# The residual of three attention blocks: DVE's multiply-add replaced by a scaled copy on ScalarE and an accumulating DMA

## What is computed

```
mod = silu(c) @ wmod                        # six vectors per batch: sa ca ga sb cb gb
h   = layernorm(x) * (1 + ca) + sa
H   = tanh(relu(rope(h @ W_Q)) + hh_b)      # "attention": projection, rotation, relu, tanh
g   = groupnorm(H, 32 groups) * gn_weight + gn_bias
x2  = x + ga * reshape(transpose(g))        # tokens and channels swapped, then read as rows
h   = layernorm(x2) * (1 + cb) + sb
y   = x2 + gb * (silu(h @ Wg) * (h @ Wu)) @ Wd     # weights looked up in a table of 16 entries
```

## Time and profile before

| | us |
|---|---|
| median of three runs | 1021.43 |
| the profiled execution, its time | 1024.31 |
| its span, first to last instruction | 1022.5 |
| TensorE busy | 929.9 (91%) |
| VectorE busy | 605.7 (59%) |
| ScalarE busy | 430.9 (42%) |
| POOL busy | 142.9 (14%) |

### The profile page before, as it was taken

The page is one execution under the profiler, slowest core; times in us unless marked ns, Lnnn a source line. Parts: engine busy times, 40 slices in busy tenths (PEclk is TensorE's granted clock), DMA queues, the critical chain, the costliest instruction groups (busy, mean ns, idle before and its releaser), DMA issues.

```text
span 1022.5 us, 12879 instructions
## 1 busy us (share of the span) xinstructions
PE 929.9 (91%) x4364; PEld 435.0 (43%) x4364; DVE 605.7 (59%) x1375; ACT 430.9 (42%) x652; POOL 142.9 (14%) x131
## 2 busy tenths in 40 slices
PE   5569678868999989999999998999999999999998
PEld 1234334333444434444444444444444444444443
DVE  5799989995899973238988863412223432222312
ACT  3375847478777732255256223222223331222200
POOL 3311202032233321121022001010000110000000
PEclk9789788989999999999999998999999999999999
DMA  8658366721001032241523305140000203000001
GB/s 280 186 123 227 83 205 167 244 63 31 21 21 31 11 124 83 72 142 34 164 51 114 83 27 200 40 146 0 0 0 1 72 31 103 0 0 0 7 35 42
DMA packets 33738, 83.44 MB, mean 82 GB/s; under 512 B 2848, under 2 KB 2976, under 8 KB 30624
## 3 DMA queue, kind: packets, MB, share of 16 engines
q1 hardware_dynamic: 32544, 74.54, 22.1%
q0 software_dynamic: 1152, 8.39, 4.4%
HBM read 64.04 MB, written 18.87 MB: 81 GB/s over the span
## 4 chain that ended last, share of the span: by engine, by line
PE 68%; DVE 17%; issue 5%; ACT 5%; DMA 3%; POOL 1%; SPq 0%; DVEq 0%; ACTq 0%
PE ps L1187 34%; PE ps L1223 22%; DVE hid L840 4%; PE ps L1154 4%; DMA xa<-x_dram 3%; PE ps L1176 2%; DVE st L759 2%; PE ps L1142 2%; PE ps L1199 2%; DVE R L826 1%; POOL work L436 1%; ACT h L500 1%; ACT xa L490 1%; PE ps L1234 1%; DVE gs L747 1%
## 5 line engine op out<-in xcount | busy, mean ns | idle before, releaser
L1187 PE MATMUL ps<-h,w_all 128*128 128x512 f16 x1920 | 418.2, 380 | 3.3 <-ACT w_all L552 2.5
L1187 PEld LDWEIGHTS ps<-h,w_all 128*128 (+1 forms) x1920 | 188.1, 98 | 230.8 <-ACT w_all L552 3.0
L1223 PE MATMUL ps<-w_all,hid 128*128 128x512 f16 x1056 | 231.9, 382 | 0.4 <-DVE w_all L1069 0.4
L1223 PEld LDWEIGHTS ps<-w_all,hid 128*128 128x128 f16 x1056 | 103.9, 98 | 125.5 <-issue 3.8
L879 DVE SCALAR_TENSOR_TENSOR hd<-ps,col,sg 128x512 f32<-128x512 f32 x80 | 59.9, 749 | 129.1 <-ACT sg L522 128.7
L522 ACT ACTIVATE sg<-ps,col 128x512 f32<-128x512 f32 x80 | 54.7, 684 | 173.4 <-PE ps L1187 173.0
L904 DVE SCALAR_TENSOR_TENSOR hd<-ps,col,gbB 128x512 f32<-128x512 f32 x32 | 24.0, 751 | 145.2 <-PE ps L1223 144.8
L1154 PE MATMUL ps<-WQ,work 128*128 128x512 f16 x384 | 87.0, 385 | 14.4 <-POOL work L436 11.2
L490 ACT ACTIVATE xa<-xa,ln_sb 128x512 f32<-128x512 f32 x60 | 43.9, 803 | 123.1 <-DVE ln_sb L769 123.1
L1176 PE MATMUL ps<-hid,w_all 128*128 128x512 f16 x352 | 85.5, 403 | 9.6 <-DVE hid L840 8.6
L537 ACT ACTIVATE hid<-hd 128x512 f16<-128x512 f32 (+1 forms) x88 | 54.8, 626 | 88.0 <-DVE hd L879 69.5
(11 more groups left out here) (113 smaller groups left out, 765.6 us busy)
## 6 DMA issues: line engine op xcount, KB each, us to landing
R<-x_dram SPq DMA_DIRECT2D x16, 1024.0 KB, 6.9
xa<-x_dram SPq DMA_DIRECT2D x14, 1024.0 KB, 5.7
hid<-idx_dram SPq DMA_DIRECT2D x44, 256.0 KB, 5.7
R<-bias_dram POOLq DMA_DIRECT2D x8, 1024.0 KB, 8.7
out_dram<-R SPq DMA_DIRECT2D x32, 256.0 KB, 2.2
x_dram<-R SPq DMA_DIRECT2D x7, 1024.0 KB, 5.1
w_all<-wmod_dram SPq DMA_DIRECT2D x6, 1024.0 KB, 12.7
h<-idx_dram SPq DMA_DIRECT2D x11, 256.0 KB, 2.6
```

Of the source, the lines that this page charges most:

```text
L1187: ins = nc.tensor.matmul(bank(GU[2 * s + t]), W[wp][:, bass.ds(at, P)], h2[hp][:, s, k], start=(k == 0 and i == 0), stop=(k == K - 1 and i ...
L1223: ins = nc.tensor.matmul(bank(QY[par]), hid[hp][:, bass.ds(at, P)], W[wp][:, w_at:w_at + BLK], start=(j == 0 and i == 0), stop=(j == J - 1 ...
```

## The change

For q = 0, 1, 2 of batch 0 the residual leaves VectorE. ScalarE copies each transposed and weighted g tile from PSUM into a buffer of its own (`bias_rows[0]`, free once the bias matrix has been stored), and POOL issues one DMA of 1 MB that accumulates this buffer onto R. The buffer is reused by the next block after that DMA has landed. `x2_ready` is now counted by ScalarE for these blocks, and SP waits for the new semaphore `g_added` (the accumulating DMA has landed) before it stores R. On POOL the accumulation of g for block q stands behind the bias addition of block q + 1. The last block of batch 0 and all of batch 1 are as before.

```diff
@@ SP
                 if not last:
-                    sp.wait_ge(x2_ready, K * (q + 1))
+                    sp.wait_ge(g_added, 16 * (q + 1))
                     sp.dma_start(x2_of_block(0, q), R[q % 2].rearrange("p (q n) -> p q n", q=A)).then_inc(x2_out, 16)
@@ POOL
             split_lo(0, hq[0], hq[1])
+            def add_g_rows(q):
+
+                pool.wait_ge(x2_ready, K * (q + 1))
+                pool.wait_ge(rows_added[q % 2], 16 * (q // 2 + 1))
+                nc.gpsimd.dma_start(R[q % 2][:], bias_rows[0], accum_op=ALU.add).then_inc(g_added, 16)
+
+            add_bias_rows(0, 0)
             for q in range(NB - 1):
-                add_bias_rows(q, 0)
                 split_lo(q + 1, hq[0], hq[1])
-            add_bias_rows(NB - 1, 0)
+                add_bias_rows(q + 1, 0)
+                add_g_rows(q)
@@ ScalarE
+            def weighted_g(q):
+
+                if q:
+                    act.wait_ge(g_added, 16 * q)
+                else:
+                    act.wait_ge(bias_out, 16)
+                for k in range(K):
+                    act.wait_ge(gt_ready, K * q + k + 1)
+                    nc.scalar.activation(bias_rows[0][:, k * C:(k + 1) * C], bank(TB[k % 2]), ACT.Copy,
+                                         scale=gnw[:, k:k + 1]).then_inc(x2_ready, 1)
...
                 if not last:
                     summed_out(w + 3, 1)
+                    weighted_g(q)
                     half_idx(w + 6, 0)
@@ VectorE
                 if last:
                     dve.wait_ge(xt_ready, K * NB)
                     dve.wait_ge(x2_out, 16 * (NB - 1))
-                residual(q, half, (xa[:, A - 1], xb[:, A - 1]) if last else ())
+                    residual(q, half, (xa[:, A - 1], xb[:, A - 1]))
```

More of the change, by code:

```diff
@@ L204, in build @@
         mod_mm = sem("mod_mm"); mod_copied = sem("mod_copied"); gate_made = sem("gate_made")
+        g_added = sem("g_added")
         silu_c = sem("silu_c"); vec_mm = sem("vec_mm"); row_mm = sem("row_mm")
```

## The result

The change made the kernel slower. The median is 1039.11 us (four runs, 1038.5 to 1044.69) against 1021.2 us before (four runs by now); the ratio is 1.0179, 95% interval 1.0151 to 1.0207, so 15 to 21 us. The forecast was 1035 us, within 1028 to 1047.

The account below looks back on a forecast made before the run. The first stage was taken to be bound by VectorE and its waits, chiefly the load of x behind the residual. Terms 6.7 + 5.8 + 1.0 = 13.5 us, added to 1021.43, gave 1035 us, within 1028 to 1047.

Parts of the forecast that it names:

- Block 1, +5.8 us: End of block 1: g lands at 137.2 behind the bias, x at 144.9, against statistics of block 3 at 139.13: +5.8 us.
- What decides: Batch 0: the residual of block q opens the way to x for block q + 2, with 0.6 us or nothing to spare.
- VectorE's relief counted at 0: Start of blocks 1 to 3: 2.90 us each off VectorE turns into waiting for the projection; paying rival 8.7 us, chance 0.03.
- Block 0, +6.7 us: End of block 0: g lands at 94.2, x at 101.9, so the statistics of block 2 wait: +6.7 us.
- Block 2, 0: End of block 2: no load of x waits for its store, 6 us in hand: 0, bound +5 if transfers collide.
- the projection of block 3, +1.0 us: Start of block 3: ScalarE's copies make TensorE's projection start later, and VectorE with it: +1.0 us.
- Sum: Whole kernel: 6.7 + 5.8 + 1.0 = 13.5 us slower.
- An accumulation from SBUF: Rival, transfers of g: a copy from SBUF is quicker than from DRAM, two blocks gain 3.0 us each, about 1029; chance 0.06.
- The collision rival: g crawls behind bias and modulation weights, x meets index loads: the stage loses 20 to 34 us, about 1047; chance 0.10.
- stall of descriptors: Rival: POOL's descriptors of g held while VectorE writes masks, each g up to 2.76 us late, about 1039; chance 0.02.

Follow-up runs that it names:

- e1: Changed kernel with the load of x for block q + 2 issued ahead of the wait for g_added: 1028.62 us, ratio 1.0085 to the kernel before.
- e3: Changed kernel without the accumulating DMA of g, ScalarE's copies kept, R stored when they are done: 1028.1 us, ratio 1.0071 to the kernel before.
- e8: e5 with the load of x still earlier, before the last index load of the block: 1016.71 us, ratio 0.9966 to the kernel before.
- e9: e2 with the load of x at the same earlier place as in e8: 1019.35 us, ratio 0.9979 to the kernel before.
- e7: Changed kernel with the modulation weights of block 1 loaded behind the load of x for block 3: 1036.27 us, ratio 1.0171 to the kernel before.
- e4: Changed kernel with POOL issuing the accumulation of g ahead of the next block's bias addition: 1043.94 us, ratio 1.0224 to the kernel before.
- e6: Changed kernel with ScalarE's weighted copies ahead of the last copy of table sums: 1036.21 us, ratio 1.0148 to the kernel before.
- e10: e1 with eight useless matmuls in TensorE's idle time between transpose groups two and three of blocks 0 to 2: 1024.34 us, ratio 1.0044 to the kernel before.
- e2: Kernel before with the load of x moved ahead of the wait for the residual: 1017.89 us, ratio 0.9974 to the kernel before.
- e5: e1 with ScalarE's weighted copies ahead of the last copy of table sums: 1022.46 us, ratio 1.0009 to the kernel before.

## Why the prediction was right, and where it was off

The mechanism and the sign came as forecast, and the time lies 4 us above the 1035. The term that was mis-sized most is the one of block 1, +5.8 us, which measured +8.94.

- *What decides.* That the load of x hangs on the residual through SP's program order, and that the change therefore puts an accumulating DMA in front of it, held: e1 and e3, which cut this link in two different ways, each take away more than half of the loss.
- *VectorE's relief counted at 0.* Right, with the cover named: the projection. Even with every wait for x gone (e8) the 2.90 us a block reappear as idle time; what may be left of them there is under 1 us in the traces and 1 to 3 us in the runs of e8 against e9.
- *Block 0, +6.7 us.* Measured +7.24. g landed after 7.8 us (8.0 assumed), x after 7.4 (7.3 assumed). ScalarE's copy out of PSUM took 0.69 us (0.73 assumed). The bias ahead of it cost nothing that shows here: it was down at 85.3, 1.3 us after the issue of g.
- *Block 1, +5.8 us.* Measured +8.94: the term that was mis-sized. I let the bias land 10 us after its issue and g about 6 us after the bias, at 137.2. The bias landed after 11.8 us and g 6.8 us behind it (2.6 us of the 3.1), and x took 7.8 instead of 7.3. The weights were on the way beside them all the while (18.4 us to land), and I had priced them at 2 us for the bias and at nothing for g. The trace of e7 shows that they are the cause: with them away and the bias still ahead, the bias took 8.4 us and g 6.9. e4 (8.0 us) had neither beside g and doesn't separate the two. That g has to wait for the bias on POOL's queue, as I wrote, isn't shown: in e6 the bias itself took longer when g came sooner behind it.
- *Block 2, 0, and the projection of block 3, +1.0 us.* No wait for the store appeared. The projection term measured 2.58 us. The later start is there (about 1 us), but I took for granted that TensorE runs at the same speed behind a pause of 2.3 us. It fell to the lower clock (0.50), and the projection took 12.20 instead of 10.52 us. e10 prices this: about 4 us by the ratios and 3 in the traces, over three blocks where they are on the path.
- *Sum.* 13.5 forecast, 17.4 between the profiled executions like for like (17.9 by medians). Of the 3.9 between, 3.1 are the transfers of block 1, 1.6 the projection of block 3, 0.5 each block 0 and the sums of block 2, less the 1.8 that the pair gets back at the feed-forward's start.
- *The rivals.* An accumulation from SBUF is not much quicker than one from DRAM (7.8 and 8.1 us against 8.0). The Trainium skill, page "DMA: Bandwidth & Descriptors", section "Anatomy of one DMA — SWDGE (gpsimd) path", has the fit from which I had estimated 4.4 us; it doesn't hold for these either. The collision rival had a core of truth in block 1 and was too dear. No stall of descriptors was seen: the issues of g in blocks 0 and 1 took 0.86 us, with VectorE idle beside them, so the rule of the Trainium skill, page "SBUF — State Buffer", section "SBUF: two separate sides", was not put to a test by g.

## What to carry to other kernels

Before work is moved off a busy engine, ask who stands behind its semaphore: here the cheap instruction was the key to a store, and behind that store, in an in-order queue, stood the load that the next block waits for. A load that needs nothing from the wait ahead of it should be issued ahead of that wait, and ahead of bulk transfers that it would share the DMA engines with; this alone was worth 2.7 us in the kernel before (e2) and 10 in the changed one (e1). And time taken from an engine is worth only what the next wait leaves of it.

## What the runs showed of the hardware

- An accumulating 1 MB DMA landed after 8.0 us with its source in DRAM (median of four, rows 10) and after 7.8 to 8.2 us with its source in SBUF (block 0 of the kernel after, e4, block 0 of e7). Two of them issued by POOL 6 to 7 us apart, with no other 1 MB transfer beside them, were both down 14.7 (kernel after), 14.8 (e6) and 13.8 us (block 1 of e7) after the first issue.
- A plain 1 MB load issued half a microsecond ahead of such a pair took 7.7 us to land in e1 and 17.2 and 17.5 in e5 and e10; issued 6 us ahead of it, 5.5 (e8). Being first by a little can't be relied on.
- A pause of 2.33 us on TensorE after short transposes was followed by a fall of the clock from 1.00 to 0.50 in some blocks (0 and 2 of the kernel after, all three of e1) and not in others (block 1 of the kernel after, block 0 of e3 and e7), at a price of 1.3 to 1.7 us each time. Pauses of 1.37 and 1.41 us at the same place in the kernel before left it at 1.00. What decides at 2.33 us these runs don't show; with matmuls in the pause (e10) it stayed at 1.00 each time.
